# Attention layers of a graph network on one core: level sums turned around, and the edge mask shared between GpSimd and VectorE

## The reference, cut to what matters

```python
def _gat_conv(x, src, dst, W, a_src, a_dst, b, n_nodes):
    h = x @ W
    alpha_s = h @ a_src
    alpha_d = h @ a_dst
    e = alpha_s[src] + alpha_d[dst]
    e = jnp.where(e > 0, e, NEG_SLOPE * e)
    m = jax.ops.segment_max(e, dst, num_segments=n_nodes)
    ...
    ex = jnp.exp(e - m[dst])
    s = jax.ops.segment_sum(ex, dst, num_segments=n_nodes)
    alpha = ex / (s[dst] + 1e-16)
    out = jax.ops.segment_sum(alpha[:, None] * h[src], dst, num_segments=n_nodes)
    return out + b
...
h = _gat_conv(x, src, dst, W1, a1s, a1d, b1, n)
h = jax.nn.relu(h)
h = _gat_conv(h, src, dst, W2, a2s, a2d, b2, n)
h = jax.nn.relu(h)
return _gat_conv(h, src, dst, W3, a3s, a3d, b3, n)
```

## Time and profile before

| | |
|---|---|
| median of 3 executions | 2073.58 us (2072.67 to 2073.6) |
| the profiled execution's own time | 2075.87 us |
| its span | 2074.0 us |
| mean granted clock of TensorE | 0.941 of full speed |
| busy over the span: PE, DVE, ACT, POOL | 81%, 72%, 56%, 54% |
| attention stage | from about 1276 to about 1923 us |
| level sums (L1637) | 1875 matmuls, 105.6 us busy |
| masks on POOL (L1541) | 375, 507.7 us busy |
| exponents on DVE (L1448) | 375, 315.8 us busy |
| bounds on DVE (L1453) | 108, 101.1 us busy |

### The profile page before, as it was taken

One profiled execution on the slowest core, in us unless ns is written; L12 is line 12 of the kernel. 1 busy time (PEld: TensorE's weight loads), 2 busy tenths in 40 slices (PEclk: granted clock), 3 DMA queues, 4 the chain that ended last, 5 costly groups with the idle time before them and its releaser, 6 DMA issues. The chain is left out here.

```text
span 2074.0 us, 36733 instructions
## 1 busy us (share of the span) xinstructions
PE 1681.0 (81%) x9771; PEld 854.7 (41%) x9772; DVE 1490.4 (72%) x3987; ACT 1158.5 (56%) x2276; POOL 1115.0 (54%) x983
## 2 busy tenths in 40 slices
PE   1777777684799999999899895799979997999675
PEld 0222222352344444444444444545344534443444
DVE  5999999435577777777777674678857896788554
ACT  5777777312344444444444442489858985898211
POOL 1000000001777777777777772399959994999200
PEclk9999999897899999999999996799989998999877
DMA  7000000101111111111111114000000000000000
GB/s 183 0 0 0 0 0 0 77 1 54 31 41 34 39 35 34 39 35 39 34 34 39 34 29 121 5 1 1 1 1 1 1 1 1 1 1 8 9 1 16
DMA packets 29632, 50.72 MB, mean 24 GB/s; under 512 B 12820, under 2 KB 13826, under 8 KB 29054
## 3 DMA queue, kind: packets, MB, share of 16 engines
q1 hardware_dynamic: 11890, 31.59, 5.1%
q0 software_dynamic: 17664, 18.12, 5.1%
HBM read 36.58 MB, written 7.39 MB: 21 GB/s over the span
## 5 line engine op out<-in xcount | busy, mean ns | idle before, releaser
L809 POOL DMA_INDIRECT adj<-h_table,l_idx x544 | 570.0, 1048 | 166.4 <-issue 157.8
L1541 POOL TENSOR_TENSOR gat_ring<-gat_ring,adj 125x750 f32<-125x750 f32 (+2 forms) x375 | 507.7, 1378 | 91.4 <-ACT gat_ring L1595 85.8
L999 DVE TENSOR_SCALAR adj<-adj,node_key 125x1024 f16<-125x1024 f16 x825 | 380.2, 503 | 203.9 <-PE psum L944 180.9
L944 PE MATMUL psum<-adj,x_sb 125*128 125x512 f16 x1650 | 403.7, 389 | 1.3 <-DVE adj L999 1.3
L1448 DVE SCALAR_TENSOR_TENSOR gat_ring<-x_sb,gat_node,psum 125x750 f32<-125x750 f32 (+2 forms) x375 | 315.8, 859 | 89.3 <-PE psum L1669 48.8
L387 PE MATMUL psum<-col_hot,src_hot 128*128 128x500 bf16 x808 | 205.6, 376 | 114.9 <-DVE src_hot L316 93.5
L872 ACT ACTIVATE l_z<-psum 128x320 f32<-128x320 f32 x204 | 89.2, 437 | 343.4 <-PE psum L923 343.3
L1666 PE MATMUL psum<-gat_ring,gat_hx 125*65 125x500 f32 (+1 forms) x500 | 250.1, 585 | 17.9 <-POOL gat_ring L1541 16.2
L721 POOL MEMSET l_aggT<- 64x3146 f32 x1 | 2.7, 2713 | 478.1 <-POOLq L1730 478.1
L313 DVE TENSOR_SCALAR col_hot<-iota_h,c_tab 128x500 bf16<-128x500 f16 x808 | 227.4, 345 | 25.1 <-PE psum L387 21.1
L1592 ACT ACTIVATE gat_ring<-gat_ring,gat_node 125x750 f32<-125x750 f32 (+2 forms) x267 | 217.7, 815 | 41.9 <-DVE gat_ring L1448 38.8
(11 more groups left out here) (241 smaller groups left out, 2080.5 us busy)
## 6 DMA issues: line engine op xcount, KB each, us to landing
adj<-h_table,l_idx POOLq DMA_INDIRECT x544, 2.6
adj<-key_table SPq DMA_DIRECT2D x33, 250.0 KB
adj<-adj SPq DMA_DIRECT2D x3, 1662.5 KB
adj_saved<-adj SPq DMA_DIRECT2D x1, 3840.3 KB
adj<-adj_saved SPq DMA_DIRECT2D x5, 688.2 KB
x_sb<-in_x SPq DMA_DIRECT2D x1, 781.2 KB
x_saved<-x_sb SPq DMA_DIRECT2D x1, 781.2 KB
out<-x_sb SPq DMA_DIRECT2D x5, 156.2 KB
```

What stands on the lines that cost most here:

```text
L809: pool.indirect_dma_start(out=to[:, t, :], out_offset=None, in_=table[:, :], in_offset=bass.IndirectOffsetOnAxis(ap=index[:, t:t + 1], axi ...
L944: last = pe.matmul(psum[:, PAIR[half] + t, :], h_parts[:, k, :], select[0:P, k % SELECTS, t * GE:(t + 1) * GE], start=(k == 0), stop=(k == ...
L999: v.tensor_scalar(select[0:P, k % SELECTS, :], keys, node_key[:, k:k + 1], None, ALU.is_equal).then_inc(s_sel, 1)
L1541: pool.tensor_tensor(slot, slot, adj[:, k, cols(c)], ALU.mult).then_inc(s["weight_ready"], 1)
```

## The change

Two things are changed, both in the attention stage.

The level sums swap their operands. The 64 levels of one k are now stationary and the columns of `adj` move, 500 and 250 at a time. Even k write the partitions 0 to 63 of PSUM and odd k the partitions 64 to 127 (`level_sums`), so that two sums side by side each hold half of the source tiles. A visit is one pair of k; there are 13 a chunk (`PAIRS`), put after products 20 to 24 and 0 to 12. VectorE limits both halves at once with limits held per partition (L1425 moves to step 17, `CLIP_AT`), the limited values go to SBUF, and `turn_levels` brings them to the target nodes with one fp32 matmul a tile against `picks`, four columns wide: the sum over the levels of either half and the two degree rows. A reduction takes the larger of the two. `picks` and `limits` are built once, by four GpSimd memsets and seven linked VectorE operations.

The mask moves to VectorE in two of five steps (n mod 5 is 1 or 3). There one operation both limits the exponential to 1 and multiplies by `adj`; ScalarE adds the score as the bias of its exponential, and neither the relu nor L1453 remains. The mask of step n stands two places behind its exponent (`MASK_LAG`).

```diff
+    def masked_by_dve(n):
+        return n % 5 in (1, 3)
...
-                if bounded_by_dve(c, k):
-                    op.then_inc(s["exponent_raw"], 1)
-                    dve.wait_ge(s["exponent_raw"], bounded_to(g, k))
-                    op = v.tensor_scalar(slot, slot, asd[:, g // GC % 2, 0, k:k + 1], 0.0, ALU.add, ALU.min)
                 op.then_inc(s["exponent_ready"], 1)
+
+            def mask(n):
+                if not masked_by_dve(n):
+                    return
+                g, k = divmod(n, NT)
+                c = g % GC
+                slot = ring[:, n % RING, 0:width(c)]
+                dve.wait_ge(s["exp_ready"], n + 1)
+                v.scalar_tensor_tensor(slot, slot, 1.0, adj[:, k, cols(c)], ALU.min, ALU.mult)\
+                    .then_inc(s["dve_weight_ready"], 1)
...
+                        if c > 0 or k >= MASK_LAG:
+                            mask(g * NT + k - MASK_LAG)
                         if c > 0 and ABSORB_AT <= k < ABSORB_AT + ops:
                             absorb(g - 1, k - ABSORB_AT)
                         if c + 1 < GC:
-                            for i in {NODE_AT - 1: (0,), NODE_AT: (1, 2), NODE_AT + 1: (3, 4, 5)}.get(k, ()):
+                            for i in {CLIP_AT: (0,), NODE_AT: (1, 2), NODE_AT + 1: (3, 4, 5)}.get(k, ()):
                                 node_step(g + 1, i)
...
                 if i == 0:
-                    op = v.tensor_scalar(mine, level_sums_of(g)[:, :, 0:WINDOWS].bitcast(I32), LOW_CODE, HIGH_CODE, ALU.max, ALU.min)
+                    op = v.tensor_scalar(by_tile(clipped[:, 0:width(g % GC)]),
+                                         pair(LEVELS_IN, 128)[:, 0:GCHUNK[g % GC], 0:P].bitcast(I32),
+                                         limits[:, 0:1], limits[:, 1:2], ALU.max, ALU.min)
                 elif i == 1:
-                    op = v.tensor_reduce(m, mine, AX.X, ALU.add)
+                    op = v.tensor_reduce(m, turned_levels(g)[:, :, 0:2], AX.X, ALU.max)
...
-                        if bounded_by_dve(c, k):
-                            act.activation(slot, slot, ACT.Exp).then_inc(s["exp_ready"], 1)
+                        if masked_by_dve(n):
+                            act.activation(slot, slot, ACT.Exp, bias=asd[:, layer % 2, 0, k:k + 1]).then_inc(s["exp_ready"], 1)
...
-                op = pe.matmul(level_sums_of(g, 128)[:, t, :], b["adj_all"][0:P, k, at:at + 128], levels[:, k, :],
-                               start=(k == 0), stop=(k == NT - 1), skip_group_check=True)
...
+                near = min(GCHUNK[c], 4)
+                for part in [slice(0, near)] + [slice(near, GCHUNK[c])] * (GCHUNK[c] > near):
+                    for k in range(2 * i, min(2 * i + 2, NT)):
+                        at = slice((GSTART[c] + part.start) * P, (GSTART[c] + part.stop) * P)
+                        last = pe.matmul(pair(LEVELS_IN, LEVELS, k % 2 * LEVELS)[:, part, 0:P], levels[:, k, :],
+                                         by_tile(adj[:, k, at]), start=(k < 2), stop=(k >= NT - 2), skip_group_check=True)
+                if i == PAIRS - 1:
+                    last.then_inc(s["levels_summed"], 1)
+
+            def turn_levels(g):
+                pe.wait_ge(s["node_rows"], 6 * g + 1)
+                for t in range(GCHUNK[g % GC]):
+                    last = pe.matmul(turned_levels(g)[:, t, :], clipped[:, t * P:(t + 1) * P], picks[:, :],
+                                     start=True, stop=True, skip_group_check=True)
+                last.then_inc(s["levels_turned"], 1)
...
+                        if k < SUMMED_AT:
+                            ahead = NT - NODE_AT if c > 0 else 0
+                            target = PAIRS * c + PAIRS * (ahead + k + 1) // (ahead + SUMMED_AT)
+                        elif k >= NODE_AT:
+                            target = PAIRS * (c + 1) + PAIRS * (k - NODE_AT + 1) // (NT - NODE_AT + SUMMED_AT)
```

More of the change, by code:

```diff
@@ L1238, in attention @@
         "adj", "psum", "ident", "x_sb", "x_flat", "aggT", "vecs", "deg", "stat", "ring", "hT", "asd", "node", "rr", "ext", "wx"))
-    levels, starts_i, starts = b["levels"], b["starts_i"], b["starts"]
+    levels, starts_i, starts, clipped, picks, limits, counts = (b[k] for k in (
+        "levels", "starts_i", "starts", "clipped", "picks", "limits", "counts"))
     codes = levels[:, :, 0:WINDOWS].bitcast(mybir.dt.int16)
@@ L1252, in attention @@
     ROW1 = 6
-    PROJECT_AT, ABSORB_AT, SUMMED_AT, NODE_AT = 6, 11, 17, 20
+    LEVELS_IN = 4
+    PROJECT_AT, ABSORB_AT, SUMMED_AT, CLIP_AT, TURN_AT, NODE_AT = 6, 11, 13, 17, 15, 20
+    MASK_LAG = 2
     WXC = D + 3
@@ L1277, in width, with dve_masks_to, pool_masks_to, pair @@
         return GCHUNK[c] * P
[L1279 to L1289, removed]
+    def masked_by_dve(n):
+        return n % 5 in (1, 3)
+    def dve_masks_to(n):
+        return sum(masked_by_dve(i) for i in range(n + 1))
+    def pool_masks_to(n):
+        return n + 1 - dve_masks_to(n)
+    def pair(bank, rows=P, first=0):
+        return psum[first:first + rows, bank:bank + 2, :].rearrange("p a b -> p (a b)").rearrange("p (t q) -> p t q", q=128)
+    def turned_levels(g):
+        return psum[0:P, LEVELS_IN + 1, 256:256 + 4 * GCHUNK[g % GC]].rearrange("p (t j) -> p t j", j=4)
     def in_psum(bank, c):
@@ L1412, in degrees_in @@
             def degrees_in(g):
-                sums = level_sums_of(g)[:, :, WINDOWS]
-                v.tensor_scalar(deg[:, tiles_of(g)], sums, -1.0, None, ALU.add).then_inc(s["degrees_read"], 1)
+                mine = counts[:, :, 0:GCHUNK[g]]
+                v.tensor_copy(mine, turned_levels(g)[:, :, 2:4].rearrange("p t j -> p j t")).then_inc(s["degrees_read"], 1)
+                dve.wait_ge(s["degrees_read"], 2 * g + 1)
+                v.scalar_tensor_tensor(deg[:, tiles_of(g)], mine[:, 0, :].bitcast(FP32), -1.0, mine[:, 1, :].bitcast(FP32),
+                                       ALU.add, ALU.add).then_inc(s["degrees_read"], 1)
             def node_step(g, i):
@@ L1436, in node_step @@
                 op.then_inc(s["node_rows"], 1)
-                if i == 0 and g < GC:
+                if i == 1 and g < GC:
                     degrees_in(g)
@@ L1482, in _ @@
             v.tensor_copy(starts[:, :], starts_i[:, :]).then_inc(s["starts"], 1)
+            link = Chain(dve, s["shift_chain"])
+            dve.wait_ge(s["constants"], 4)
+            for half in range(2):
+                last_row = ident[:, half * LEVELS + WINDOWS:half * LEVELS + LEVELS]
+                link(v.tensor_tensor(picks[:, half:half + 1], picks[:, half:half + 1], last_row, ALU.subtract))
+                link(v.tensor_copy(picks[:, 2 + half:3 + half], last_row))
+            link(v.tensor_tensor(limits[:, 0:1], picks[:, 0:1], picks[:, 1:2], ALU.add))
+            link(v.tensor_scalar(limits[:, 1:2], limits[:, 0:1], HIGH_CODE - COUNT_CODE, COUNT_CODE, ALU.mult, ALU.add))
+            link(v.tensor_scalar(limits[:, 0:1], limits[:, 0:1], LOW_CODE, None, ALU.mult))
             weight_columns(1)
@@ L1486, in _ @@
             first_features()
-            link = Chain(dve, s["shift_chain"])
             for layer in range(LAYERS):
@@ L1504, in _ @@
                         if c + 1 < GC:
-                            for i in {NODE_AT - 1: (0,), NODE_AT: (1, 2), NODE_AT + 1: (3, 4, 5)}.get(k, ()):
+                            for i in {CLIP_AT: (0,), NODE_AT: (1, 2), NODE_AT + 1: (3, 4, 5)}.get(k, ()):
                                 node_step(g + 1, i)
+                for n in range((first + GC) * NT - MASK_LAG, (first + GC) * NT):
+                    mask(n)
                 for i in range(ops):
@@ L1523, in _ @@
             pool.memset(levels[:, :, WINDOWS:LEVELS], 1.0).then_inc(s["constants"], 1)
+            pool.memset(picks[:, :], 0.0).then_inc(s["constants"], 1)
+            pool.wait_ge(s["constants"], 2)
+            for half in range(2):
+                pool.memset(picks[half * LEVELS:(half + 1) * LEVELS, half:half + 1], 1.0).then_inc(s["constants"], 1)
+            pool.wait_ge(s["constants"], 4)
             pool.wait_ge(s["agg_transposed"], NC)
@@ L1698, in _ @@
                 first = layer * GC
-                for i in range(GCHUNK[0] * NT):
-                    level_sum(first, i)
+                for i in range(PAIRS):
+                    level_sums(first, i)
+                turn_levels(first)
                 row2(first)
                 row1(first)
-                coming = [(first + c, i) for c in range(1, GC) for i in range(GCHUNK[c] * NT)]
+                coming = [(first + c, i) for c in range(1, GC) for i in range(PAIRS)]
                 taken = 0
```

59 lines of the change are left out of this document (31 added, 28 removed).

## The result

The changed kernel takes 2091.68 us (median of 4 runs, 2087.99 to 2093.57) beside 2073.12 for the kernel before: ratio 1.0088, 95% interval 1.0071 to 1.0106. It is slower, by 18.6 us; the prediction was 2091. The profiled run took 2090.9 us, its span is 2089.1.

A forecast was written before the change was run, and what follows sets the result against it. TensorE was taken as the bound in six-tile chunks. A layer: 8.2 + 2.9 + 1.4 - 3 x 1.6 - 2.5 = +5.2 us; three layers +15.6, once +1.4: +17.0 on 2073.58, 2091 us; own range 2076 to 2105, overall 2056 to 2136.

The forecast's parts named there:

- The likeliest case: Level sums' halves run side by side but each visit loses 0.19 us to changeover: 2091 us in all, chance 0.40.
- The visit: Level sums on TensorE: 0.32 us streaming plus 0.19 lost at entry and exit (bounds 0 and 0.27); +8.2 us a layer.
- The turns: 22 matmuls a layer turning sums back in chunks 1 to 4, 0.13 us each: 2.9 us in full, lower bound 0.7.
- The stalls: TensorE loses 3.6 us per six-tile chunk; the masks on VectorE return 1.6 of it, bounds nothing to 3.6.
- Chunk 4: 500 columns, no level sums, VectorE bounds: masks save 25 x 0.10 = 2.5 us a layer.
- The layer's start: First level sums, limit, reduction and three turns, covered by nothing: +1.4 us a layer, upper bound +5.3.
- The preamble: Seven linked tiny VectorE operations, once, before the first features: +1.4 us.
- rival 4: Everything balances: stalls of 3.6 us come back, turns are covered, the changeover halves: 2070 to 2078 us, chance 0.05.
- 1, a free changeover: The 0.19 us a visit belongs to L933's fp32 weights, so 156 visits give 29.6 us back: 2061 us, chance 0.28.
- 2, halves in line: The two column halves of a level-sum visit run one after another: +57 us, 2148 us, chance 0.15.
- 3, VectorE through the port: VectorE becomes the bound through the port shared with GpSimd, each mask waiting 0.8 us: 2115 us, chance 0.12.

The follow-up runs named there:

- experiment 3: Changed kernel with all source tiles but k = 1 in the lower column half, so no two level sums run side by side: 2131.86 us, ratio 1.0283.
- experiment 4: Changed kernel with four source tiles a visit, seven visits a chunk in place of thirteen, same matmuls: 2077.33 us, ratio 1.0026.
- experiment 5: Changed kernel with each level sum's stationary operand 128 wide, so no chunk matmul is 64 wide (result differs from the reference): 2102.08 us, ratio 1.0139.
- experiment 7: Changed kernel with one turning matmul a chunk in place of one a tile (other tiles' shifts wrong): 2089.55 us, ratio 1.0071.
- experiment 1: Kernel before with only the masks' part, two of five masks on VectorE, level sums as before: 2057.3 us, ratio 0.9931.
- experiment 2: Changed kernel with only the level sums' part, masks and bounds as before: 2096.8 us, ratio 1.0119.
- experiment 6: Changed kernel with VectorE's mask reading row 1 in PSUM, not the adjacency in SBUF (two steps in five unmasked): 2088.46 us, ratio 1.0071.

## Why the prediction was right, and where its steps were off

**Total and mechanism: right.** The likeliest case, halves side by side but a changeover at each visit, is what the trace shows, and experiments 3, 4 and 5 separate its two parts. The forecast of 2091 met 2091.68 with several terms off in opposite directions.

**The visit: mis-sized.** Booked 0.32 + 0.19 = 0.51 us; it is 0.32 + 0.27 = 0.59, with the changeover at the upper bound that I had named. Over 39 visits of six tiles a layer that is 3 us more. The 0.19 from the earlier trace rows held the step into the 64-wide operand and out of it, but it was what remained of 3.13 us after three sums of columns times a price; a distance between two starts, with and without the visit, would have been the surer measure.

**The turns: right in their lower bound, wrong in the sum.** One costs 0.21 us and not 0.13, because I divided by its count of records, which is twice the matmuls. Booked in full as 2.9 us a layer, they are worth at most 0.9 (experiment 7), all of it at the layer's start, where single starts scatter by as much: the cover was VectorE and its shifts, not ScalarE as I wrote.

**The stalls: the step that was most wrong.** I took 3.6 us of a six-tile chunk for lost. With row matmuls and projections at 0.22 us, TensorE's demand before was 25 x 1.467 + 18 x 0.22 = 40.6 us of 42.7, so only 2.1 were lost. And I credited the masks with 1.6 of them. Alone they return 2.6 us over a layer's three six-tile chunks, 0.9 in each (experiment 1); on top of the new level sums they return nothing there (experiment 2). The level sums had removed these stalls already by making TensorE slower than GpSimd: 25 x 1.26 + 13 x 0.59 + 24 x 0.21 = 44.2 of 45.2 us. Two parts of a change that relieve the same wait must not both be booked.

**Chunk 4: right**, -2.6 us a layer against -2.5, in each kernel with the masks.

**The layer's start: too low.** +2.6 us, not +1.4. Over the three layers the first group takes 0.4 us more on the mean (4.1 against 3.75). The row matmuls, which the change does not touch, take 1.0 more, because TensorE's clock is at 0.50 for them and was at 1.00 before in two of three layers: a term that I did not have. The turns (0.82 to 1.42 us) and the wider limit, less the shorter reduction, make the rest. The starts scatter by 1 us between layers and kernels.

**The preamble: right where it stands, not booked to its end.** The seven tiny operations take 1.3 us on VectorE, and the first features come 1.3 us later after the stage's first matmul (5.95 us against 4.62). But the first level codes come only 0.2 us later after the stage's first instruction (34.4 against 34.2): something else was the last there.

**The range and rival 4: sums that do not come out.** By my own terms the range's lower end was 2066 and not 2076: stalls returned in full are 9 x 2.0 = 18 us less, turns covered 3 x 2.2 = 6.6. With half the changeover too, rival 4 would have been 2052 and not 2070 to 2078.

**In order of size**, a layer: level sums, turns and start were booked at +12.5 and add 11.7 on top of experiment 1; the masks were booked at -7.3 and give -5.0 alone. Sum booked +5.2, measured +6.7. That the total met the forecast to 0.7 us is partly luck: the three layers cost 20 us where I had booked 15.6, and in the profile the stages ahead happened to be 3.5 us shorter and the preamble all but vanished.

**Rivals.** 1, a free changeover: refuted; experiment 5's full width has none, the 64-wide form has 0.27 us. 2, halves in line: refuted by experiment 3. 3, VectorE through the port: the contention exists, it stretches GpSimd's masks by 0.2 us at 750 columns and VectorE's by as much at 500, and the time hangs on it by 3 us at most, within the scatter (experiment 6).

## What to carry to other kernels

Packing two narrow operands beside each other halves the streaming, but each trip between that form and full width has a price (0.27 us here), so it wants long groups: with the same matmuls, two tiles a visit made the whole change 0.9% slower and eight 0.3% faster. Even so it was not worth having here, since the masks alone gave 0.7%. Price a thing inserted into a stream from the distance between starts with and without it, and find out what a count counts before dividing by it. When a change has two parts, time each alone: here one half was worth -15 us and the other +24.5, the pair +18.6, which hides the gain and is not their sum. And where nothing covers TensorE, look at its clock before and after: here the changed work ahead of them left the row matmuls at the lower level, 2.88 us and not 1.57.

## What the runs showed that I had not expected

- At the step into a 64-wide operand and out of it no weight load ran ahead of its matmul (idle before it "issue", 0.30 to 0.37 us, same start as the matmul); with a 128-wide one the load began 0.21 us early, and inside a 64-wide visit the later loads run ahead too.
- The time hung strongly on a mask's place in VectorE's queue: one position later cost 75 us over 150 masks, 0.5 us each, one earlier about 22 us in all, by the ratios.
- Of two masks that meet, the one that starts second is stretched: GpSimd's from 1.57 to 2.02 us where it came second at 750 columns, VectorE's from 0.67 to 1.01 where it came second at 500, and a six-column operation of VectorE from 0.16 to 1.59.
- Untouched row matmuls cost 1.0 us a layer more, because the clock stayed at its lower level; in experiment 3, with a longer group ahead of them, they were back at 1.57 us.
